# The edge loop of a graph layer: one load for sixteen list positions, the row of destinations issued earlier, two buffers for the lists

## The reference

```python
hh = (x @ W).reshape(n, H, D)
s_src, s_dst = einsum(hh, a_src), einsum(hh, a_dst)
scores = leaky_relu(s_src[src] + s_dst[dst], 0.2)
e = exp(scores - segment_max(scores, dst)[dst])
msgs = hh[src] * (e / segment_sum(e, dst)[dst])[:, :, None]
out = segment_sum(msgs, dst) + x            # then layernorm, elu
...
gate_logits = x @ gate_w + gate_b           # 16 experts, the best two
topk_vals, topk_idx = top_k(gate_logits, 2)
expert_out = relu(x @ w1 + b1) @ w2 + b2    # of the two, weighted by softmax
```

## Time and profile before

| what | value |
|---|---|
| median of three runs | 3192.68 us |
| the profiled execution | 3186.81 us |
| its span (first to last instruction) | 3185.1 us |
| edge loop, first `num` of the loop to the last | 326.15 to 2616.11 us |
| PE, DVE, ACT, POOL busy | 1771.6, 1754.0, 1115.8, 1871.5 us |
| DMA, mean over the span | 123 GB/s |

### The profile page before, as it was taken

The page is one execution under the profiler, slowest core; times in us unless marked ns, Lnnn a source line. Parts: engine busy times, 40 slices in busy tenths (PEclk is TensorE's granted clock), DMA queues, the critical chain, the costliest instruction groups (busy, mean ns, idle before and its releaser), DMA issues. The chain is left out here.

```text
span 3185.1 us, 43688 instructions
## 1 busy us (share of the span) xinstructions
PE 1771.6 (56%) x9011; PEld 1444.0 (45%) x9012; DVE 1754.0 (55%) x4247; ACT 1115.8 (35%) x2079; POOL 1871.5 (59%) x1936
## 2 busy tenths in 40 slices
PE   6343545455454545445454545554454555899994
PEld 5232434343343434334343434343343434799993
DVE  6544546455554646555554645455564645665655
ACT  3323333333333333333333333342333332343433
POOL 2356666666666666666666666666666651555555
PEclk9667777776777777777777778777777767999997
DMA  5433344443434344343434444343443436433336
GB/s 189 114 114 111 108 127 122 111 125 109 127 110 128 107 125 126 110 127 107 125 110 124 122 113 124 110 125 107 129 123 110 125 97 207 127 106 99 107 104 247
DMA packets 185080, 393.00 MB, mean 123 GB/s; under 512 B 50833, under 2 KB 107626, under 8 KB 178772
## 3 DMA queue, kind: packets, MB, share of 16 engines
q0 software_dynamic: 90864, 262.34, 29.1%
q1 hardware_dynamic: 77524, 115.84, 11.8%
q10 hardware_dynamic: 16656, 14.43, 2.0%
HBM read 355.94 MB, written 36.52 MB: 123 GB/s over the span
## 5 line engine op out<-in xcount | busy, mean ns | idle before, releaser
L1267 POOL DMA_INDIRECT gat<-table,idx x1627 | 1546.8, 951 | 905.1 <-issue 471.7
L1366 PE MATMUL ps_sum<-msg,hot 128*128 128x264 f32 x3322 | 1097.6, 502 | 709.7 <-DVE msg L1413 449.1
L1366 PEld LDWEIGHTS ps_sum<-msg,hot 128*128 128x128 f32 x3322 | 829.7, 256 | 920.3 <-issue 726.3
L1413 DVE TENSOR_TENSOR msg<-gat,ps_weight 128x2304 f32<-128x2304 f32 x196 | 472.0, 2408 | 564.3 <-ACT ps_weight L1324 359.0
L1279 ACT ACTIVATE hotT<-dst_row,neg_id 128x4352 bf16<-128x4352 int16 x48 | 188.2, 3921 | 518.0 <-DMA dst_row<-dst_half 485.4
L1352 PE MATMUL ps_look<-dst_split,hotT 128*128 (+1 forms) x1661 | 80.8, 191 | 500.2 <-ACT hotT L1281 368.3
L1352 PEld LDWEIGHTS ps_look<-dst_split,hotT 128*128 128x128 bf16 x1661 | 67.2, 101 | 517.8 <-issue 489.3
L1566 DVE TENSOR_TENSOR num<-acc,ps_sum 128x264 f32<-128x264 f32 x49 | 21.0, 429 | 438.7 <-remote 241.9
L1410 DVE TENSOR_TENSOR hot<-ps_own,rel 128x1152 f32<-128x1152 f32 x196 | 250.2, 1277 | 0.0
L1324 ACT ACTIVATE ps_weight<-score 128x72 f32<-128x72 f32 x196 | 44.1, 225 | 508.7 <-DVE score L1404 494.8
L2130 PE MATMUL ps_ht<-xT,w_t 128*128 128x128 f32 x1712 | 214.5, 280 | 0.0
(11 more groups left out here) (412 smaller groups left out, 2135.4 us busy)
## 6 DMA issues: line engine op xcount, KB each, us to landing
dst_row<-dst_half SPq DMA_DIRECT2D x49, 1088.0 KB
gat<-table,idx POOLq DMA_INDIRECT x1661
b_t<-in_L_ffn_b_dram ACTq DMA_DIRECT2D x107, 128.0 KB
listing<-list_f SPq DMA_DIRECT2D x736, 0.5 KB
table<-rows SPq DMA_DIRECT2D x49, 128.0 KB, 1.7
y_rows<-y SPq DMA_DIRECT2D x48, 128.0 KB
x_all<-in_x_dram SPq DMA_DIRECT2D x6, 896.0 KB, 8.8
back<-chosen SPq DMA_DIRECT2D x3, 1792.0 KB, 17.6
```

Source lines behind the costliest of these rows:

```text
L1267: pool.indirect_dma_start(gat[:, GSTART[g] + k, :], None, table, bass.IndirectOffsetOnAxis(ap=idx[g][:, k:k + 1], axis=0)).then_inc(landed ...
L1366: made = pe.matmul(ps_sum[:, 0:SUM], hot[:, m, k, :], msg[:, m, k, :], start=(g == 0 and k == 0), stop=(g == NG - 1 and k == n - 1))
L1413: dve.tensor_tensor(msg[:, m, 0:n, 0:D].rearrange("p j (h d) -> p j h d", d=HD), gat[:, j:j + n, 0:D].rearrange("p j (h d) -> p j h d", d=HD),
```

## The change

On SP a register load no longer has an assertion behind it; the order of a turn is edges, y, row, gates, lists in place of row, edges, y, gates, lists; the row waits on `apart_ready` (the first of ACT's two passes, the only one that reads the row) in place of `hotT_ready`; the sixteen positions come with one load; and `record` has a further wait on `listed`. On ACT `rows(t+1)` stands at the end of the turn. On PE `look(t+1, 0)` stands behind `total(t, 3)`. `base_i` and `list_f` have two buffers.

```diff
--- before.py
+++ after.py
@@ -1226,7 +1226,7 @@
         @block.sync
         def _(sp):
             def window(t):
-                return sp.value_load(lo_i[0:1, bass.ds(t, 1)], min_val=0, max_val=E)
+                return sp.value_load(lo_i[0:1, bass.ds(t, 1)]).with_bounds(min_val=0, max_val=E)
 
             def edges(t):
                 lo = window(t)
@@ -1236,14 +1236,19 @@
                     sp.dma_start(edges_i[i * WCH:(i + 1) * WCH, :],
                                  v[bass.ds(lo, WIN)].rearrange("(r e) -> r e", e=P)).then_inc(edges_in, 16)
 
+            def row(t):
+                lo = window(t)
+                sp.wait_ge(apart_ready, t)
+                sp.sem_inc(sp_turn, 1)
+                sp.dma_start(dst_row[:, :], dst_half[bass.ds(lo, WIN)].unsqueeze(0).to_broadcast([P, WIN])).then_inc(row_in, 16)
+
             def tile(t, head, old, last=False):
-                if not head:
-                    lo = window(t)
-                    sp.wait_ge(hotT_ready, t)
-                    sp.sem_inc(sp_turn, 1)
-                    sp.dma_start(dst_row[:, :], dst_half[bass.ds(lo, WIN)].unsqueeze(0).to_broadcast([P, WIN])).then_inc(row_in, 16)
                 if not last:
                     edges(t + 1)
+                if old >= 3:
+                    finish.keep(sp, t - 3, sp_turn)
+                if not last:
+                    row(t + 1)
                 if old >= 3:
                     finish.record(sp, t - 3, sp_turn)
 
@@ -1316,8 +1321,6 @@
                         finish.lower(act, t - 1)
                     if g == 2 and old >= 2:
                         finish.odds(act, t - 2)
-                    if g == NG - 1 and not last:
-                        rows(t + 1)
                     act.wait_ge(score_ready, t * NG + g + 1)
                     if not (head and g < 2):
                         act.wait_ge(sum_done, t * NG + (g - 1))
@@ -1327,6 +1330,7 @@
                         sources(t + 1, g)
                 if not last:
                     relative(t + 1)
+                    rows(t + 1)
 
             over_tiles(act, tile)
             finish.norm_inner(act, FULL)
@@ -1373,8 +1377,6 @@
                 for g in range(NG):
                     if g < NG - 1:
                         look(t, g + 1, head, last)
-                    elif not last:
-                        look(t + 1, 0, False)
                     if g == 1 and old >= 2:
                         finish.vote(pe, t - 2, ps_route)
                     total(t, g, head, last)
@@ -1384,6 +1386,8 @@
                         finish.ranks(pe, t - 2, ps_route)
                     if g == 2 and old >= 2:
                         finish.fill(pe, t - 2, ps_route)
+                if not last:
+                    look(t + 1, 0, False)
 
             pe.wait_ge(finish.gate_in, 32)
             look(0, 0, True)
@@ -1504,12 +1508,12 @@
         self.rsum = sb("rsum", [P, 2])
         self.pick, self.hit = sb("pick", [P, 2, EXPERTS]), sb("hit", [P, 2, EXPERTS])
         self.both, self.both_h = sb("both_f", [P, EXPERTS]), sb("both_h", [P, EXPERTS], BF16)
-        self.base, self.base_i = sb("base", [P, EXPERTS]), sb("base_i", [P, EXPERTS], I32)
+        self.base, self.base_i = sb("base", [P, EXPERTS]), sb("base_i", [P, 2, EXPERTS], I32)
         self.base_f, self.at_f, self.at_i = sb("base_f", [P, EXPERTS]), sb("at_f", [P, 2]), sb("at_i", [P, 2], I32)
         self.spots_ready, self.put = sem("spots_ready"), sem("put_l")
         self.rank, self.lane = sb("rank", [P, 2]), sb("lane", [P, P])
         self.named, self.spots = sb("named", [P, 2, EXPERTS]), sb("spots", [P, 2, P])
-        self.list_f = sb("list_f", [EXPERTS, P])
+        self.list_f = sb("list_f", [EXPERTS, 2, P])
         self.ready, self.par_in, self.gate_in = sem("finish_consts"), sem("par_in"), sem("gate_in")
         self.sum_done, self.added = sem("sum_done"), sem("added")
         self.xn_ready, self.var1_ready, self.std1_ready = sem("xn_f_ready"), sem("var1_ready"), sem("std1_ready")
@@ -1521,6 +1525,7 @@
         self.both_ready, self.ranks_done = sem("both_f_ready"), sem("ranks_done")
         self.entries, self.list_done, self.list_ready = sem("entries"), sem("list_done"), sem("list_ready_f")
         self.sent, self.listed = sem("sent"), sem("listed")
+        self.records = 0
         self.gates_ready, self.gates_out = sem("gates_ready"), sem("gates_out")
         self.turn_taken = turn_taken
 
@@ -1638,15 +1643,15 @@
         dve.tensor_tensor(self.named[:, :, :], self.pick[:, :, :],
                           one(self.ids[:, bass.ds(a, 1), :]).unsqueeze(2).to_broadcast([P, 2, EXPERTS]),
                           ALU.mult).then_inc(self.entries, 1)
-        if not (isinstance(a, int) and a == 0):
-            dve.wait_ge(self.listed, a * (16 * EXPERTS))
-        link(dve.tensor_tensor(self.base_i[:, :], self.base[:, :], self.expert_row[:, :], ALU.add))
+        if not (isinstance(a, int) and a < 2):
+            dve.wait_ge(self.listed, (a - 1) * (16 * EXPERTS))
+        link(dve.tensor_tensor(one(self.base_i[:, bass.ds(a & 1, 1), :]), self.base[:, :], self.expert_row[:, :], ALU.add))
         link(dve.tensor_tensor(self.base[:, :], self.base[:, :], ps_route[:, 2 * EXPERTS:3 * EXPERTS], ALU.add))
         dve.tensor_tensor(self.spots[:, :, :], iota.unsqueeze(1).to_broadcast([P, 2, P]),
                           self.rank[:, :].unsqueeze(2).to_broadcast([P, 2, P]), ALU.is_equal).then_inc(self.entries, 1)
 
-    def spots_of_listed(self, dve, link):
-        link(dve.tensor_copy(self.base_f[:, :], self.base_i[:, :]))
+    def spots_of_listed(self, dve, link, a):
+        link(dve.tensor_copy(self.base_f[:, :], self.base_i[:, a & 1, :]))
         link(dve.tensor_tensor(self.hit[:, :, :], self.base_f[:, :].unsqueeze(1).to_broadcast([P, 2, EXPERTS]),
                                self.pick[:, :, :], ALU.mult))
         link(dve.tensor_reduce(self.at_f[:, :], self.hit[:, :, :], AX.X, ALU.add))
@@ -1674,7 +1679,7 @@
 
     def hand_over(self, dve, a, ps_route):
         dve.wait_ge(self.list_done, a + 1)
-        dve.tensor_copy(self.list_f[:, :], ps_route[0:EXPERTS, LIST_AT:LIST_AT + P]).then_inc(self.list_ready, 1)
+        dve.tensor_copy(one(self.list_f[:, bass.ds(a & 1, 1), :]), ps_route[0:EXPERTS, LIST_AT:LIST_AT + P]).then_inc(self.list_ready, 1)
 
     def norm_inner(self, act, a):
         if not (isinstance(a, int) and a == 0):
@@ -1750,13 +1755,18 @@
         sp.dma_start(self.y_rows[bass.ds(a * P, P), D:YROW], one(self.gates[:, bass.ds(a, 1), :])).then_inc(self.gates_out, 16)
 
     def record(self, sp, a, turn):
-        self.keep(sp, a, turn)
         sp.wait_ge(self.list_ready, a + 1)
         sp.sem_inc(turn, 1)
         self.keep_gates(sp, a)
+        if not (isinstance(a, int) and a == 0):
+            sp.wait_ge(self.listed, a * (16 * EXPERTS))
+            sp.sem_inc(turn, 1)
+        regs = [sp.alloc_register(name=f"list_at{self.records}_{e}") for e in range(EXPERTS)]
+        self.records += 1
+        sp.load(regs, one(self.base_i[0:1, bass.ds(a & 1, 1), :]))
         for e in range(EXPERTS):
-            at = sp.value_load(self.base_i[0:1, e:e + 1], min_val=0, max_val=DROWS - P)
-            sp.dma_start(self.lists[bass.ds(at, P)].unsqueeze(0), self.list_f[e:e + 1, :]).then_inc(self.listed, 16)
+            at = sp.snap(regs[e], donate=True).with_bounds(min_val=0, max_val=DROWS - P)
+            sp.dma_start(self.lists[bass.ds(at, P)].unsqueeze(0), one(self.list_f[e:e + 1, bass.ds(a & 1, 1), :])).then_inc(self.listed, 16)
 
 
 def load_weights(eng, q, w1, w2, w1_sb, w2_sb, w_in):
@@ -1896,7 +1906,7 @@
             finish.scale_inner(dve, link, b)
             finish.scale_outer(dve, link, a)
             finish.affine(dve, link, ps_affine)
-            finish.spots_of_listed(dve, link)
+            finish.spots_of_listed(dve, link, a - 1)
             finish.lift(dve, link, b)
             dve.tensor_copy(before_late[:, :], base[:, :])
             dve.tensor_copy(region[:, 0:EXPERTS], finish.expert_row[:, :])
```

## The result

The kernel after took 3386.89 us (median, 3382.16 to 3398.38), the kernel before 3197.92 in the same job: a ratio of 1.0586 (95% interval 1.0556 to 1.0615). It is slower, where 3189 us was forecast, and above the range for 8 in 10, which ended at 3265. It is near the 3412 us of rival C, which I had given 0.10.

What follows compares the result with a forecast made beforehand. POOL's 34 gathers plus semaphore stops, 51.0 us a tile, were taken as the bound; 3186.81 + 45 × 0 − 1 = 3186 us profiled, 3192 by the median, 3189 given; 8 in 10 range 3015 to 3265.

Steps and rivals of the forecast that it cites:

- rival C: POOL, half of group 3: total's signal seen, look's not, POOL runs on; 5.0 us a tile lost, 3412 us; chance 0.10.
- What bounds the kernel: Edge loop: POOL's gathers and stops, 51.0 us a tile, are the bound, not the row's chain to ACT.
- PE's signals are seen only after POOL has stopped: While POOL streams gathers, PE's semaphore is not seen; it comes a few us after POOL's stop.
- `total(t,3)` 9 us ahead of the stop: 0: PE's total(t,3) ends 9 us ahead of POOL's stop instead of 5, signal still seen at 2160.2: gain 0.
- PE, look behind total: 0, bounds 0.5 gained to 4.8 lost: look(t+1,0) ends about 39 us behind num, DVE reads it at 51: 0, from 0.5 us gained to 4.8 lost.
- ACT: Both hotT passes behind the last exp: PE's last group 33 us behind num, not 43; msg 4.0 us sooner; gain 0.
- SP: One load, no assertions: sixteen lists take 8 to 12 us, not 24.91, beside POOL's 51 us: gain 0.
- The pieces (D): Lists as 256 pieces a tile: 0 in the sum; as slower rival 1.2 us a tile, 3241 us; chance 0.16.
- The end: Last tile, total(t,3) not behind a hotT: a gain of 0 to 2 us, 1 of it in the sum.
- The rule of the Trainium skill, "SBUF — State Buffer": Says PE and ACT never wait on anyone; the prediction read it as about data ports, not signals.
- Rival B: The row's chain ahead of ACT's hotT is the bound; without it 2920 us, to POOL's floor 2810; chance 0.08.

Runs made afterwards that it cites:

- f3: Kernel after with a further POOL wait for look_done at the half of group 3, late job: 3203.54 us, 1.0050 of the kernel before.
- g2: Kernel before with SP's parts and the two buffers alone, ACT and PE in the old order, prompt job: 2759.38 us, 1.0003 of before.
- e1: Kernel after with look(t+1,0) ahead of total(t,3) on PE again, prompt job: 2846.14 us, 1.0321 of the kernel before.
- e4: Kernel after with one list_f buffer again, so lists are written whole, prompt job: 2759.75 us, 1.0005 of the kernel before.
- e2: Kernel after with a further POOL wait for look_done at the half of group 3, prompt job: 2760.35 us, 1.0003 of the kernel before.
- e3: Kernel before with SP's parts and the two buffers alone, same kernel as g2, another prompt job: 2760.28 us, 1.0009 of before.
- g3: Kernel before with PE's order alone, look(t+1,0) behind total(t,3), prompt job: 2758.08 us, 0.9996 of the kernel before.
- the g job: The job that ran g1, g2, g3 and the kernel before with a pause on POOL (2996.04 us, 1.0860); signals were prompt.
- the k job: Late job with the kernel after unchanged, 3353.57 us (1.0545 of before), and g1's kernel, 3343.18 us (1.0426).
- g1: Kernel after with SP's row back in the old place behind the lists, prompt job: 2759.36 us, 1.0002 of the kernel before.
- f2: Kernel before, unchanged, profiled in a late job: 3189.76 us, 51.2 us a tile.

## Why the prediction was wrong

- *What bounds the kernel*: the row's chain is not the bound. Right: the 485.4 us of ACT went and nothing was gained, in late jobs (f3) and in prompt ones (g2).
- *PE's signals are seen only after POOL has stopped*: too strong as a rule, and read from turns that are not the usual ones. Two turns could not tell "held until the stop" from "seen some microseconds late, or at the stop". In 30 of the 45 turns of before POOL had stopped already when `total(t,3)` ended; the turn of the earlier trace rows is one, with total over at 1442.20 and POOL's last gather at 1441.19:

```profile
1435.79 6.41 PE L1366 MATMUL ps_sum<-msg,hot 128*128 128x264 f32 x16 [1.75 <-issue]
```

  In the other 15 total ended at most 5.3 us ahead of the stop. In after it mostly ends 14 to 17 us ahead of it, and DVE acts on it 2 to 10 us behind its end, within the stream.
- *`total(t,3)` 9 us ahead of the stop: 0*. This step failed. I took the signal's arrival as pinned to the stop, at 2160.2. It moved, and with it the stop itself: in the turn shown `num` starts 4.7 us behind the end of total and 11.6 us ahead of the end of POOL's last gather, POOL does not stop at the half of group 3, and look's signal, held until 4.2 us behind POOL's later stop, opens the turn late.
- *PE, look behind total: 0, bounds 0.5 gained to 4.8 lost*. This is the term with the wrong value: it was put at 0 and measured 4.9 us a tile (55.8 against 50.9), just beyond the bound for a loss. The chance of that, 0.10, came from holding both signals to the same stop. In C itself the working of one turn held: the stop ahead of group 0 was to end 9.5 us behind POOL's last gather and ended 10.1 behind it. That the mean comes so near to C's 5.0 is partly luck: C had every turn lose that much, and 39 lost more while six gained.
- *ACT*: PE's last group was to start 33 us behind `num`. It starts 32.1 us behind the reduce that opens the turn (2028.32 against 1996.2), but that reduce is now 13.8 us behind `num`, which makes 45.9. The working inside the turn was right; the sign that I had named, 33 behind `num`, did not come.
- *SP*: sixteen lists were to take 8 to 12 us. In the turn shown they take 17.54, so this was mis-sized for a late job; in a prompt one it was right, as in e1. Either way they lie beside other work, as said.

```profile
1474.79 11.78 SPq L1769 DMA_DIRECT2D listing<-list_f  x16
```

- *The pieces (D)*: no time was lost to them, as forecast: e4, without them, is no faster than e2 and e3. The engine time is there, though. In e2, with pieces, and e4, with whole lists, the hardware queue takes 14.0% and 13.6% of the span, and the queue of POOL's gathers, with the same packets, 35.4% and 33.5%:

```profile
q0 software_dynamic: 90864, 262.34, 35.4%
q1 hardware_dynamic: 99124, 115.88, 14.0%
```

```profile
q0 software_dynamic: 90864, 262.34, 33.5%
q1 hardware_dynamic: 77524, 115.84, 13.6%
```

  Summed over the packets of both queues e2 takes 979 us more of engine time, 21.8 for each of the 45 turns, where I had worked out 18.6; most of it is in packets of gathers and not in those of lists. The packets themselves rose by 21600, which is 30 for each of 720 lists, where I had counted 15.
- *The end*: a gain of 2 us was measured behind the last `num`, as said; ahead of the loop 15.6 us were gained that I had not looked for.
- *The rule of the Trainium skill, "SBUF — State Buffer"*: what I weighed it against, a release 8 us behind PE's last matmul, is real in late jobs and absent in prompt ones (0.1 us in g3). Rival B, which I had tied to it, did not come in either.

What stays open. First, whether it is POOL's stream that holds the signals. The pause that would test it only ran in prompt jobs. What the traces do show is a connection in late jobs. I take sum_done and look_done of all eight late traces together, and call gathers with less than 0.45 us between them a stream. Of the signals whose last matmul ended in the first 3 us of a stream, 316 of 472 came within 0.3 us; of those that ended more than 6 us into one, 30 of 1598. With POOL idle for over 2 us it was 111 of 117. A stream alone does not do it: in g3, a prompt job, POOL streams for 2035 us without a stop and all 196 sum_done come at once. Second, why total's signal passes within the stream and look's, 2.7 us behind it, does not. Third, what makes a job late. It is not the chip: the g job and the k job ran on one and the same and were prompt and late (the record does not tell whether on the same core). All three late jobs had the kernel after among their kernels and no prompt one had; three and five are too few to call it a cause, and it means that the kernel after itself has no prompt time. Its nearest relatives have (e4, 1.0005; g1, 1.0002). No version beat the kernel before on either kind. Of the four with the change that ran in a late job f3 comes nearest, 0.5% slower there and equal where signals are prompt (e2). SP's parts alone and PE's order alone ran in prompt jobs only, so what each of them does in a late one is not measured.

## What to carry to other kernels

A wait that is "never last" can still be the thing that makes an engine stop at a useful point. When a signal is moved earlier, ask which engine will now run through the place where it used to stop, and who else was served by that stop. If two signals are needed by the same consumer and only one is asked for at a gate, ask for both there: that one wait was worth 147 us of 3350 in a late job, and cost nothing in a prompt one. And when a reading says "A is seen only when B stops", price the case that A is seen a little sooner before calling it free.

## What the runs showed of the hardware

The same program took 2758 us in one job and 3188 us in another, 16% more. Of the 430 us, 389 lie in the 45 turns (42.6 against 51.2 us a tile in g3 and f2) and 41 ahead of them, in a stretch that has the first turns of the edge loop. With it goes the delay between a matmul and its signal: counted from the start of a group's last matmul it is 0.40 us in every one of 196 groups in a prompt job (g3), and 4.3 us on average with a longest of 23.5 in the late trace of before (a rough figure, as that trace has 177 records of the signal for 196 groups). The time of one job does not tell that there are two kinds of it; that delay, read from the trace, does, and it is worth reading first.
